# Attention and a top-1 mixture of experts on one core: rows that carry their token's number, the scaling of the second weights on GpSimd, and a new order of work

## The reference

```python
x = L0_attn_input_data                              # (2, 2048, 128) f32: two sequences, 4096 tokens
xn = layernorm(x)                                   # no gain, no bias, eps 1e-5
# attention, one head of width 128, causal
scores = einsum('bsd,de,bte->bst', xn, qk, xn) / sqrt(128), masked by tril
attn = einsum('bst,btd,de->bse', softmax(scores), xn, ov)
# mixture of 8 experts, each token goes to the one whose centroid it likes best
aff = xn @ centroids.T
eid = argmax(aff)
alpha = sigmoid(sum(xn * centroids[eid]))
xln = layernorm(xn) * ln_g[eid] + ln_b[eid]
ffn = relu(xln @ w1[eid] + b1[eid]) @ w2[eid] + b2[eid]     # 128 -> 512 -> 128
return x + attn + xn + alpha * ffn
```

## Time and profile before

| | |
|---|---|
| three runs | 278.7, 275.29, 276.15 us |
| median | 276.15 us |
| profiled execution | 271.44 us |
| its span in the trace | 269.7 us |
| mean granted clock of TensorE | 0.928 of full speed |
| TensorE busy | 226.2 us (84%) |
| VectorE busy | 179.1 us (66%) |
| ScalarE busy | 157.2 us (58%) |
| GpSimd busy | 112.5 us (42%) |

### The profile page before, as it was taken

One profiled execution on the slowest core, in us unless ns is written; L12 is line 12 of the kernel. 1 busy time (PEld: TensorE's weight loads), 2 busy tenths in 40 slices (PEclk: granted clock), 3 DMA queues, 4 the chain that ended last, 5 costly groups with the idle time before them and its releaser, 6 DMA issues.

```text
span 269.7 us, 6880 instructions
## 1 busy us (share of the span) xinstructions
PE 226.2 (84%) x2450; PEld 169.4 (63%) x2450; DVE 179.1 (66%) x469; ACT 157.2 (58%) x354; POOL 112.5 (42%) x158
## 2 busy tenths in 40 slices
PE   8899799799999495513999999789779687999995
PEld 5643457667787262102686789578668586777774
DVE  6999999988989232013999795545325442447975
ACT  4999897734888342004576655335335343878883
POOL 8384889600046776772000002553553555340000
PEclk9689999979999977555999999999999999999999
DMA  6971507990001111111920004435334411009335
GB/s 196 310 187 42 155 1 168 149 145 6 0 10 44 49 43 47 59 50 46 152 58 4 2 1 100 119 90 127 75 86 110 89 32 41 32 30 272 86 114 157
DMA packets 41296, 23.48 MB, mean 87 GB/s; under 512 B 12424, under 2 KB 39088, under 8 KB 41264
## 3 DMA queue, kind: packets, MB, share of 16 engines
q1 hardware_dynamic: 38656, 18.24, 30.6%
q0 software_dynamic: 2272, 4.67, 5.3%
q10 hardware_dynamic: 336, 0.14, 0.2%
HBM read 11.15 MB, written 9.34 MB: 76 GB/s over the span
## 4 chain that ended last, share of the span: by engine, by line
PE 53%; issue 15%; DVE 12%; ACT 8%; another core or an unknown queue 7%; DMA 2%; SPq 1%; DVEq 0%; ACTq 0%
PE psum L1377 4%; PE psum L1376 4%; PE psum L1353 4%; PE psum L1378 4%; PE psum L1410 4%; PE psum L1427 4%; PE psum L1419 4%; PE psum L1420 4%; PE psum L1514 3%; PE psum L1512 2%; PE psum L1539 2%; PE psum L1540 2%; PE psum L1513 2%; PE psum L1538 2%
## 5 line engine op out<-in xcount | busy, mean ns | idle before, releaser
L697 POOL DMA_INDIRECT sorted_y<-xn,store x39 | 37.9, 971 | 78.8 <-ACT xn L1236 67.9
L1097 ACT ACTIVATE p_sb<-psum 128x512 f32<-128x512 f32 (+1 forms) x80 | 42.0, 533 | 10.9 <-PE psum L1410 6.1
L1065 DVE SCALAR_TENSOR_TENSOR h_lo<-psum,h_hi 128x512 f16<-128x512 f32 x39 | 26.3, 688 | 32.5 <-ACT h_hi L1228 23.7
L1091 ACT ACTIVATE p_hi<-psum 128x512 f16<-128x512 f32 (+3 forms) x56 | 30.6, 547 | 28.8 <-PE psum L1427 13.4
L687 POOL DMA_INDIRECT sorted_x<-xr,pos x32 | 32.0, 999 | 36.3 <-issue 33.2
L951 DVE TENSOR_TENSOR p_lo<-p_sb,p_hi 128x512 f16<-128x512 f32 (+3 forms) x56 | 34.2, 615 | 13.1 <-ACT p_sb L1097 11.5
L1228 ACT ACTIVATE h_hi<-psum 128x512 f16<-128x512 f32 x39 | 23.2, 600 | 33.7 <-PE psum L1514 20.3
L1353 PE MATMUL psum<-kT_hi,qT_hi 128*128 128x512 f16 (+3 forms) x80 | 26.0, 361 | 14.0 <-DVE row_max L932 8.0
L936 DVE TENSOR_REDUCE row_max<-psum 128x1 f32<-128x512 f32 x48 | 31.6, 682 | 5.0 <-PE psum L1353 5.0
L1376 PE MATMUL psum<-qT_hi,kT_hi 128*128 128x512 f16 (+1 forms) x80 | 28.9, 361 | 3.0 <-issue 1.8
L1539 PE MATMUL psum<-w_hl,h_hi 128*128 x156 | 28.3, 219 | 3.3 <-issue 3.3
(11 more groups left out here) (211 smaller groups left out, 561.5 us busy)
## 6 DMA issues: line engine op xcount, KB each, us to landing
w_raw<-in_L_ffn_w SPq DMA_DIRECT2D x16, 256.0 KB, 3.3
sorted_x<-zero SPq DMA_DIRECT2D x1, 2515.5 KB, 20.0
xn<-sorted_x SPq DMA_DIRECT2D x8, 258.0 KB, 4.8
x_sb<-in_L_attn_input_data SPq DMA_DIRECT2D x8, 256.0 KB, 5.4
xn<-sorted_y SPq DMA_DIRECT2D x8, 256.0 KB, 5.1
out<-x_sb SPq DMA_DIRECT2D x6, 256.0 KB, 2.6
sorted_y<-xn,store POOLq DMA_INDIRECT x39, 2.3
sorted_x<-xr,pos POOLq DMA_INDIRECT x32
```

What stands on the lines that cost most here:

```text
L697: pool.indirect_dma_start(out=sorted_y[:, :], out_offset=bass.IndirectOffsetOnAxis(ap=store[:, t:t + 1], axis=0), in_=xs[:, t % SLOTS, 0:P ...
L1097: a.activation(p_sb[:, u, off:GW], bank[SCORE[n % R]][:, off:GW], ACT.Exp, scale=SCALE).then_inc(s_exp, 1)
```

## The change

A row in `sorted_x` is now 130 floats: the alpha at column 128 (WEIGHT), and at column 129 (TOKEN) the number of the token, an integer. GpSimd writes the numbers once with an iota into the rows to be sent, and numbers of unused rows of sorted_y into the four copies of the zero row. `clear_rows` fills sorted_x with these by four DMAs, each of every fourth tile. The scatter of results takes its indices from the rows themselves. So the search from places to tokens is left out: OHK, OHC, OHP, INV, FIN and the last four operations of PL, with the constants, the bank and the semaphores for them. In W2, ScalarE now makes the high half in one pass with a scale of 16, and GpSimd's W2l has a product by 16 in place ahead of the subtraction. The list ORDER is another one throughout; a line of either stands for it here.

```diff
@@ -66,68 +66,67 @@
 ORDER = entries("""
-VAR.0.1 PICK LE.0.1 LE.1.2 MISC C0a WU VAR.1.2 C0 AE.0 RN.0.1 AE.1 C1 ROW.0.1 C1a RN.1.2 C1v ROW.1.2 T.0 Ta.0 AE.2 T.1
...
+WU MISC VAR.0.1 LE.0.1 VAR.1.2 C0 C1 C2 T.0 T.1 BIASa LE.1.2 RN.0.1 RN.1.2 RN.2.3 BASE.0 BASE.1 BASE.2 RN.3.4 RN.4.8
...
-BANKED = ("T", "Q", "V", "W1", "M", "SH", "AFF", "CNT", "INVA")
+BANKED = ("T", "Q", "V", "W1", "M", "SH", "AFF", "CNT")
...
-    N_CONST = N_EARLY + 10
+    N_CONST = N_EARLY + 6
...
-    SPARE = 14
+    DUMPS = 4
     APART = 3
     KF = 6
-    PLACES_BY_ACT = (1, 3, 5, 7)
-    PLACES_BY_DVE = tuple(q for q in range(8) if q not in PLACES_BY_ACT)
+    ROW = P + 2
+    WEIGHT, TOKEN = P, P + 1
...
-        sorted_rows = bass.AP(sorted_x.bitcast(F32).tensor, 0, [[P + 1, NS * P], [1, P + 1]])
-        sorted_halves = bass.AP(sorted_x.tensor, 0, [[2 * P + 2, NS * P], [1, 2 * P]])
+        sorted_rows = bass.AP(sorted_x.bitcast(F32).tensor, 0, [[ROW, NS * P], [1, ROW]])
+        sorted_halves = bass.AP(sorted_x.tensor, 0, [[2 * ROW, NS * P], [1, 2 * P]])
...
             def clear_rows():
 
                 sp.wait_ge(s_zero, 1)
-                sp.dma_start(sorted_rows.rearrange("(p r) d -> p r d", p=P),
-                             zero[:, :].bitcast(F32).unsqueeze(1).broadcast_to([P, NS, P + 1])).then_inc(s_zeroed, 16)
+                sp.wait_ge(s_dump, 1)
+                by_place = sorted_rows.rearrange("(t p) d -> p t d", p=P)
+                for k in range(DUMPS):
+                    tiles = len(range(k, NS, DUMPS))
+                    sp.dma_start(by_place[:, k:NS:DUMPS, :], zero[:, k:k + 1, :].bitcast(F32).broadcast_to([P, tiles, ROW])
+                                 ).then_inc(s_zeroed, 16)
...
-                    sp.wait_ge(s_yst[t % SPARE], 16 * (t // SPARE + 1))
+                    sp.wait_ge(s_yst[t % DUMPS], 16 * (t // DUMPS + 1))
...
             def routing_constants():
                 pool.memset(tile_e[:], 0).then_inc(s_const, 1)
-                for dst, first, step, n, per_p in ((tile_no[:], 0, 1, NS, 0), (token_tile[:], 0, 1, NT, 0),
-                                                   (partition[:], 0, 0, 1, 1), (columns, 0, 1, P, 0)):
-                    pool.iota(dst, pattern=[[step, n]], base=first, channel_multiplier=per_p,
-                              allow_small_or_imprecise_dtypes=True).then_inc(s_const, 1)
-                for first in range(0, NS, SPARE):
-                    n = min(SPARE, NS - first)
-                    pool.iota(spare[:, first:first + n], pattern=[[P, n]], base=N, channel_multiplier=1,
-                              allow_small_or_imprecise_dtypes=True).then_inc(s_spare, 1)
+                pool.iota(column(zero[:, :, 2 * TOKEN:2 * ROW].bitcast(I32)), pattern=[[P, DUMPS]], base=N,
+                          channel_multiplier=1).then_inc(s_dump, 1)
+                pool.iota(column(xr[:, :, 2 * TOKEN:2 * ROW].bitcast(I32)), pattern=[[P, NT]], base=0,
+                          channel_multiplier=1).then_inc(s_token, 1)
...
                 if i == 0:
                     pool.wait_ge(s_index, 1)
                     pool.wait_ge(s_weight, 1)
-                    pool.wait_ge(s_zeroed, 16)
+                    pool.wait_ge(s_zeroed, 16 * DUMPS)
+                    pool.wait_ge(s_token, 1)
...
             def store_rows(t):
                 pool.wait_ge(s_ysb, t // FT + 1)
-                if t == 0:
-                    pool.wait_ge(s_store, 1)
-                wait(pool, s_yst[t % SPARE], 16 * (t // SPARE))
                 transfer_before()
-                pool.indirect_dma_start(out=sorted_y[:, :], out_offset=bass.IndirectOffsetOnAxis(
-                    ap=store[:, t:t + 1], axis=0), in_=xs[:, t % SLOTS, 0:P], in_offset=None).then_inc(s_yst[t % SPARE], 16)
-                transfers.append((s_yst[t % SPARE], 16 * (t // SPARE + 1)))
+                tokens = xs[:, t % SLOTS, TOKEN:ROW].bitcast(U32)
+                pool.indirect_dma_start(out=sorted_y[:, :], out_offset=bass.IndirectOffsetOnAxis(ap=tokens, axis=0),
+                                        in_=xs[:, t % SLOTS, 0:P], in_offset=None).then_inc(s_yst[t % DUMPS], 16)
+                transfers.append((s_yst[t % DUMPS], 16 * (t // DUMPS + 1)))
...
                     pool.wait_ge(s_w2hi, e + 1)
                     rows_first(job)
+                    pool.tensor_scalar(w2_raw[:, e % RW, :], w2_raw[:, e % RW, :], W_SCALE, None, ALU.mult).then_inc(s_w2s, 1)
+                    pool.wait_ge(s_w2s, e + 1)
                     pool.tensor_tensor(out=w2_hl[:, e, F:2 * F], in0=w2_raw[:, e % RW, :], in1=w2_hl[:, e, 0:F],
                                        op=ALU.subtract).then_inc(s_w2lo, 1)
...
-                place_link(v.tensor_scalar(tile_of[:], posf[:], 1.0 / P, 0.5 / P - 0.5, ALU.mult, ALU.add))
-                place_link(v.tensor_scalar(tile_of[:], tile_of[:], 3.0 * 2.0 ** 22, None, ALU.add))
-                place_link(v.tensor_scalar(tile_of[:], tile_of[:], 3.0 * 2.0 ** 22, None, ALU.subtract))
-                v.scalar_tensor_tensor(out=place_in[:], in0=tile_of[:], scalar=-float(P), in1=posf[:],
-                                       op0=ALU.mult, op1=ALU.add).then_inc(s_pos, 1)
-
-            def hot_tiles():
-                wide = [P, NT, NS]
-                v.tensor_tensor(hot_k[:, :, 2, :], tile_no[:].unsqueeze(1).broadcast_to(wide),
-                                tile_of[:].unsqueeze(2).broadcast_to(wide), ALU.is_equal).then_inc(s_hot, 1)
-                v.wait_ge(s_hot, 1)
-                v.tensor_tensor(hot_k[:, :, 0, :], hot_k[:, :, 2, :], token_tile[:].unsqueeze(2).broadcast_to(wide),
-                                ALU.mult).then_inc(s_hot, 1)
-
-            def hot_places(q):
-                v.wait_ge(s_pos, 1)
-                wait(v, s_inv, q - 1)
-                for i in range(GT):
-                    ins = v.tensor_scalar(hot_p[:, q % 2, i, :], columns, place_in[:, q * GT + i:q * GT + i + 1], None,
-                                          ALU.is_equal)
-                ins.then_inc(s_hotp, 1)
-
-            def find_tokens():
-                at = bank[bank_of["INVA",]][:, 0:3 * NS].rearrange("p (c k) -> p c k", c=3)
-                v.wait_ge(s_inv, NG)
-                v.wait_ge(s_spare, 3)
-                v.tensor_copy(token_f[:], at[:, 1, :]).then_inc(s_find, 1)
-                v.wait_ge(s_find, 1)
...
-                v.tensor_copy(store[:], spare_f[:]).then_inc(s_store, 1)
...
-                v.tensor_scalar(column(xr[:, :, 2 * P:2 * P + 2].bitcast(F32)), alpha[:], 1.0 / (W_SCALE * W_SCALE), None,
+                v.tensor_scalar(column(xr[:, :, 2 * WEIGHT:2 * TOKEN].bitcast(F32)), alpha[:], 1.0 / (W_SCALE * W_SCALE), None,
                                 ALU.mult).then_inc(s_weight, 1)
...
-                    a.activation(w2_raw[:, u, :], w2_raw[:, u, :], ACT.Copy, scale=W_SCALE).then_inc(s_w2s, 1)
-                    a.wait_ge(s_w2s, e + 1)
-                    a.activation(w2_hl[:, e, 0:F], w2_raw[:, u, :], ACT.Copy).then_inc(s_w2hi, 1)
+                    a.activation(w2_hl[:, e, 0:F], w2_raw[:, u, :], ACT.Copy, scale=W_SCALE).then_inc(s_w2hi, 1)
...
-                if kind == "OHC":
-                    a.wait_ge(s_const, N_CONST)
-                    a.wait_ge(s_hot, 1)
-                    a.activation(hot_k[:, :, 1, :], hot_k[:, :, 2, :], ACT.Copy, scale=partition[:, 0:1]).then_inc(s_hotc, 1)
-                if kind == "OHP" and job[1] in PLACES_BY_ACT:
-                    q, k = job[1], PLACES_BY_ACT.index(job[1])
-                    a.wait_ge(s_const, N_CONST)
-                    a.wait_ge(s_pos, 1)
-                    wait(a, s_hota, k)
-                    for i in range(GT):
-                        ins = a.activation(far[:, i, :], columns, ACT.Square, scale=-1.0,
-                                           bias=place_in[:, q * GT + i:q * GT + i + 1])
-                    ins.then_inc(s_far, 1)
-                    a.wait_ge(s_far, k + 1)
-                    wait(a, s_inv, q - 1)
-                    a.activation(hot_p[:, q % 2, :, :], far, ACT.Relu, scale=-1.0, bias=onesf[:, 0:1]).then_inc(s_hota, 1)
...
-                                       scale=xs[:, t + i, P:P + 1])
+                                       scale=xs[:, t + i, WEIGHT:TOKEN])
...
-            def tokens_of_places(q):
-                at = bank[bank_of["INVA",]][:, 0:3 * NS]
-                if q in PLACES_BY_ACT:
-                    pe.wait_ge(s_hota, PLACES_BY_ACT.index(q) + 1)
-                else:
-                    pe.wait_ge(s_hotp, PLACES_BY_DVE.index(q) + 1)
-                if q == 0:
-                    pe.wait_ge(s_hot, 2)
-                    pe.wait_ge(s_hotc, 1)
-                for i in range(GT):
-                    t = q * GT + i
-                    m = mm(at, hot_p[:, q % 2, i, :], hot_k[:, t, :, :].rearrange("p c k -> p (c k)"), start=(t == 0),
-                           stop=(t == NT - 1))
-                m.then_inc(s_inv, 1)
```

183 lines of the change are left out of this document (70 added, 113 removed).

## The result

On its first chip the changed kernel took 282.4 us in the median of four runs (277.34 to 285.81), the kernel before 275.7 (273.51 to 278.7): a ratio of 1.033, 95% interval 1.021 to 1.045. It is slower, by 6.7 us, where 271.0 us was forecast, about 5 us less than before. Two later measurements beside the kernel before gave 1.035 (1.025 to 1.044) and 1.015 (1.004 to 1.025). Medians here are over all runs, while ratios with an interval compare only the fast runs of each kernel, those within about 1.5% of its fastest.

The account below looks back on a forecast made before the run. VectorE was taken to bound the front, no engine 88 to 126 us, where scatters slow the others. Terms -2.3 - 0.5 - 2.0 - 1.6 - 1.8 + 3.1 = -5.1 took 276.15 to 271.0 us, range 262 to 281.

Parts of the forecast that it names:

- step X.26: The 27th score step on TensorE, at 82.94 us in the kernel before; forecast to come 6 us earlier.
- The scatters: Token-row scatters on GpSimd: six pass freely, 26 cost TensorE 0.87 us each; -1.8 us, bounds -8.8 and +5.5.
- Rival (a): Row scatters without interposed operations all cost 1.15 us: +12.4 in place of -1.8, 285.3 us in all; chance 0.13.
- The result scatters: Expert part: 1.7 more bursts of four result scatters, 1.83 us of TensorE idle each; +3.1 us, bounds 0 and +5.5.
- The search: Between 66 and 91 us, removing the token search's 32 matmuls saves TensorE time: -2.3 us, bounds -1.7 and -3.4.
- The front: New order early on: VectorE's subtractions move behind the last group's maxima, -2.0 us; slow clock after the hole goes, -1.6.
- the hole at 80: TensorE's idle time at 80 to 82 us, beside VectorE's comparisons, goes with the search: -0.5 us.
- The hole of 50 to 55 us: TensorE busy 3.46 of 5.00 us while VectorE is full; forecast to go, with the slow clock behind it.
- on an engine that then has slack: 0: VectorE's moved subtractions beside GpSimd's new products may stretch by 1.7 us in all, counted as costing nothing.
- rival (b): The front gains nothing, held by ScalarE's queue: -1.0 us, 275.2 in all; sign under 5 us gained before scatters; chance 0.22.
- The scaling of weights: ScalarE loses 8 passes of 0.62 us, GpSimd gains 8 products of 1.16 us; the extra 9 us lie under cover.
- A dead stretch that moves costs nothing by itself: Row scatters starting about 5 us later than 77.63 us cost nothing; some 25 us of room before the expert part.

Follow-up runs that it names:

- a_same: The changed kernel unaltered, run again as reference beside three variants on chip C: 281.7 us against 273.5 for the kernel before, ratio 1.035.
- a_reorder: The changed kernel with ScalarE's highs and results of the expert part in the sequence of the kernel before: 277.1 us, 1.020 of the kernel before.
- b_w2pool: The kernel before with only the scaling of the second weights by 16 moved from ScalarE to GpSimd: 271.0 us against 266.7, ratio 1.017.
- a_tiny: The changed kernel with a one-column GpSimd memset, waited for, after every fourth row scatter: 237.8 us against 232.7 for the kernel before, ratio 1.028.
- a_pause8: The changed kernel with a 128x512 GpSimd product by 1 after every eighth row scatter: 240.7 us against 232.7 for the kernel before, ratio 1.035.
- a_breaks: The changed kernel with three GpSimd weight jobs back among the row scatters, where the kernel before had them: 272.7 us, 1.003 of the kernel before.
- a_pause: The changed kernel with a 128x512 GpSimd product by 1 after every fourth row scatter: 266.3 us, 0.978 of the kernel before.
- a_best: The changed kernel with earlier clearing of sorted_x, seven GpSimd breaks among row scatters and the old sequence of results: 255.7 us against 271.2 before, ratio 0.947.

## Why the prediction was wrong, by its own steps

**Where the miss lies.** The profiled execution is 5.9 us longer where 5.1 less was forecast, a miss of 11.0. By the marks that the prediction set, 3.7 of it come up to step X.26 (2.3 us earlier, not 6), 4.2 from there to the first operation of the experts (2.0 us longer, where 2.2 shorter was left of the sum), and 3.1 behind it (6.2 longer, not 3.1). No single term makes the whole.

**The step that failed** is "The scatters": "26 x 0.87 = 22.6 against 24.4, -1.8". It took a price per scatter, in which the breaks had no part. The trace gave +3.9 us of idle time in the stretch of the row scatters (a_same's more, 29.6 against 21.5). From X.26 to the experts TensorE lost 31.4 us (27.0 idle, 4.4 slow clock) against 27.3 (21.3 and 6.0), so +4.0 with the clock. The runs show why: with three breaks put back the kernel was 9.0 us faster. The sum had a slip too. From 88.00 us on the kernel before has 26 scatters and not 28, since two other operations of GpSimd were counted with them. Both kernels then have 26 behind the first six, 24.4 us make 0.94 each, and a fixed price gives no gain at all.

Rival (a), "without the pauses that the three interposed operations gave", 0.13, had the mechanism that the breaks bear out, but not its price. Its sign was 30 us or more of idle and slow clock between the seventh scatter and the last; the trace has 23.9 (21.2 and 2.7), near the 22 of the forecast, and before has 22.7 between the same two. That its 285.3 us lies only 2.9 us from the measurement is luck, as the last paragraphs of this section show. The clue had been read and left aside: the only good part (97 to 103 us) came behind a break. That the first six pass freely held (TensorE nearly full from 80 to 97 us); what follows them had no fixed price.

**The result scatters** (+3.1, bounds 0 and +5.5): right in direction, but not steady in size. The trace has +3.9 us of idle time and 1.6 of slow clock, 5.5 together, the end of the bounds. Bursts of three or more scatters 1.26 us apart are nine in it and five before; bursts of four are three in either, not seven. a_reorder gives 4.5 back. On chip B, without the row scatters, the same two sequences differ by only 1.0 us of idle and slow clock (14.3 against 13.3).

**The search** (-2.3 to -3.4) is gone with its 2.9 us of matmuls. **The front** (-2.0 and -1.6, with -0.5 for the hole at 80): mis-sized. The hole of 50 to 55 us and its slow clock did go, but a new one came from 20 to 30 us, with the clock at 0.66 after. The term that failed there is "on an engine that then has slack: 0", for VectorE's work beside the new products of GpSimd: its eight operations took 3.5 us longer, on the queue that TensorE waits for. The scaling alone accounts for 0.8 of it (b_w2pool), and the rest came only with the new order beside it. Without row scatters, the first result scatter came at 129.9 us against 133.1: 3.2 us for all that stands ahead of the experts, against 6.4 in the sum. By its sign, less than 5 us gained up to the scatters, rival (b) came true, and its -2.3 for the search alone is near. Its mechanism did not come: TensorE has no idle time from 40 us to X.26, where ScalarE's exponentials 15 to 20 would have held it.

**The scaling of weights** was not all under cover, as the 4 us of b_w2pool and its share of the 3.5 us above say, and the profile prices the product higher than the 1.16 us taken:

```profile
L713 POOL TENSOR_SCALAR w_raw<-w_raw 128x512 f32<-128x512 f32 x8 | 12.4, 1553 | 1.1 <-ACT w_hl L1115 0.5
```

The first scatter at 84.73 was forecast at 80 to 84; it waits for the clearing, whose transfers take 10.3 and 12.1 us:

```profile
sorted_x<-zero SPq DMA_DIRECT2D x3, 650.0 KB, 10.3
...
sorted_x<-zero SPq DMA_DIRECT2D x1, 585.0 KB, 12.1
```

"A dead stretch that moves costs nothing by itself" held only where engines starve. Where they do not, the later scatters are what the experts wait for (a_tiny, a_pause8); the changed kernel itself was not run there, and a_tiny, with breaks of 0.1 us, is the nearest to it.

**The forecast time.** 271.0 against 282.4, and 281 as the range's end. Had the scatter term been rival (a)'s +12.4, the sum would have been 285.3; with the front's 3.2 in place of 6.4 it would be 288.5, some 6 above the measurement. So rival (a)'s 1.15 us for each of 32 scatters is too much: 25.4 us of idle time and 2.6 of slow clock in the changed kernel's trace make 28.0, 0.88 each.

Not settled: what in the chip lets one engine's indirect DMAs hold back the instructions of three others, whether it is their issuing or their transfers, and why on some chips only. That it is a port of SBUF is not shown. That the engines wait for their own instructions is a rival that no run tests; against it, between 92 and 131 us the changed kernel's trace has only two packets of instructions, of 8 KB, the later at 125.3 us, and ScalarE goes on only at 130.64.

## What to carry to other kernels

Before indirect DMAs of GpSimd are put in one row, look at what the other engines do beside them in a trace, and where they stop, keep useful GpSimd operations of 1.5 us or more between groups of four or so. Ask the same of VectorE's operations beside new work of GpSimd: here eight of them took 5.84 us in place of 2.35. The work to be hidden behind them must be placed so that the last transfer is still early: breaks pay only while others starve, and cost their length where they do not. When the same kernel differs by a sixth between chips, judge a change on both kinds.

## What the runs showed of the hardware

- On chips A, B, C and E TensorE is idle 21.5 to 29.6 us in the 44 to 52 us of the row scatters, in every trace with these scatters but a_breaks, a_pause and a_best. VectorE and ScalarE stand still with it, in waits that nothing in the trace ends. The scatters are 1.26 us apart there. Their own length is 0.96 to 0.98 us on either kind of chip. On D TensorE was idle 0.45 us over 50 us of the same scatters, on F 1.4 us over 62, besides its wait for the last rows.
- The result scatters cost TensorE 9.5 to 15 us of idle time on the first kind and 0.3 to 0.6 on the second.
- The first five to eight scatters of a run hold nobody back. Breaks of 1.5 us and more restore most of that, breaks of 0.1 us do not.
- Eight normalising operations of VectorE (128x127, float32) took 2.35 us where GpSimd was idle beside most of them, 3.1 with a product of GpSimd more beside them, and 5.8 to 5.9 with GpSimd busy throughout.
- A 128x512 float32 product by a constant on GpSimd took 1.55 us in the mean, longer than the subtraction of two such tiles, 1.16.
